# Mamba mixer with gated mixture of experts: tap order, output projection and work moved to GpSimd

## What is computed

```
def _mamba2_layer(h, Wi, cw, cb, dtb, Alog, Dh, gw, Wo):
    z, xBC, dt = split(h @ Wi)
    xBC = silu(cb + sum(xp[:, k:k + L, :] * cw[:, k] for k in range(4)))
    xs, Bm, Cm = split(xBC)
    dt = softplus(dt + dtb)
    hs = hs * exp(dt * A) + dt * xs * B     # per token, a scan
    y = (hs . C) + D * xs
    return rmsnorm(y * silu(z), gw) @ Wo

for l in range(4):
    h = h + _mamba2_layer(_rmsnorm(h, block_norm_w[l]), ...)
```

## Time and profile before

| | us |
|---|---|
| runs | 1157.63, 1160.88, 1161.12 |
| profiled execution, time | 1162.99 |
| profiled execution, span | 1161.0 |
| mean granted TensorE clock | 0.952 of full speed |
| busy PE, DVE, ACT, POOL | 993.7, 977.1, 884.2, 676.3 |

### The profile page before, as it was taken

How to read it: one execution, slowest core, us unless ns; L and a number is a source line. 1 busy time by engine, 2 the same in 40 slices (tenths; PEclk the granted TensorE clock), 3 DMA queues, 4 the chain that set the end, 5 groups by cost and what they waited for, 6 DMA issues and landing times.

```text
span 1161.0 us, 25184 instructions
## 1 busy us (share of the span) xinstructions
PE 993.7 (86%) x6136; PEld 559.7 (48%) x6136; DVE 977.1 (84%) x1801; ACT 884.2 (76%) x1724; POOL 676.3 (58%) x853
## 2 busy tenths in 40 slices
PE   5799999999899999999999999985788767999980
PEld 4244544445444444454445444542444445777760
DVE  6779999999999999999999998974778775888865
ACT  5688999999899999999999999984556534655640
POOL 0267577766776677656655765672244551666661
PEclk9789999999999999999999999998888888999995
DMA  5111242224222432210001000100000115676638
GB/s 141 34 34 33 89 156 86 88 87 153 91 86 87 142 102 86 78 32 22 22 23 31 22 22 23 27 7 1 19 28 28 37 33 180 223 232 226 223 116 217
DMA packets 85584, 97.84 MB, mean 84 GB/s; under 512 B 20698, under 2 KB 65888, under 8 KB 85536
## 3 DMA queue, kind: packets, MB, share of 16 engines
q1 hardware_dynamic: 80544, 88.83, 24.2%
q0 software_dynamic: 4992, 8.48, 2.2%
HBM read 59.67 MB, written 37.83 MB: 84 GB/s over the span
## 4 chain that ended last, share of the span: by engine, by line
PE 35%; DVE 26%; issue 18%; ACT 6%; POOL 3%; DVEq 2%; DMA 1%; ACTq 0%; SPq 0%; POOLq 0%
DVE cv L1354 9%; PE bank L494 4%; PE bank L562 4%; PE bank L681 2%; PE bank L667 2%; DVE M L1370 2%; PE bank L683 2%; PE bank L682 2%; DVE cv L1350 2%; PE bank L619 2%; PE bank L693 2%; PE bank L695 2%; PE bank L692 2%; PE bank L658 2%; PE bank L640 2%
## 5 line engine op out<-in xcount | busy, mean ns | idle before, releaser
L1354 DVE SCALAR_TENSOR_TENSOR cv<-bank,PAR,cv 128x511 f32<-128x511 f32 (+2 forms) x384 | 274.1, 742 | 15.7 <-ACT cv L963 2.8
L1370 DVE SCALAR_TENSOR_TENSOR M<-E,bank 128x512 f32<-128x512 f32 x256 | 168.3, 678 | 20.7 <-ACT E L951 11.4
L1679 POOL TENSOR_TENSOR yt<-yt,ti 128x384 f32<-128x384 f32 x64 | 64.0, 1000 | 203.6 <-DVE ti L1470 203.6
L494 PE MATMUL bank<-hn,WA 128*128 128x512 f32 x256 | 144.9, 649 | 41.0 <-DVE cv L1354 40.6
L951 ACT ACTIVATE E<-bank 128x512 f32<-128x512 f32 x256 | 149.0, 595 | 31.9 <-DVE M L1370 30.1
L1710 POOL DMA_INDIRECT RS<-y,XR x92 | 98.8, 1074 | 78.7 <-DVE y L1567 55.4
L1703 POOL DMA_INDIRECT XS<-stage,IDX x64 | 65.9, 1029 | 79.2 <-DVE run L1329 62.1
L1101 ACT ACTIVATE hr<-bank,W1B 128x512 f32<-128x512 f32 x92 | 63.4, 689 | 56.7 <-PE bank L683 49.8
L562 PE MATMUL bank<-M,dtx 128*32 128x128 f32 x2048 | 82.9, 279 | 15.6 <-DVE o_sb L1389 15.1
L494 PEld LDWEIGHTS bank<-hn,WA 128*128 128x128 f32 x256 | 40.6, 194 | 111.9 <-issue 74.0
L1497 DVE TENSOR_TENSOR hL<-hr,hH 128x512 fp32r<-128x512 f32 x124 | 87.1, 702 | 4.3
(11 more groups left out here) (245 smaller groups left out, 2633.8 us busy)
## 6 DMA issues: line engine op xcount, KB each, us to landing
XS<-PADT SPq DMA_DIRECT2D x32, 520.0 KB, 4.3
WA<-w_in SPq DMA_DIRECT2D x192, 64.0 KB, 1.8
W1B<-WD SPq DMA_DIRECT2D x23, 514.0 KB
W2B<-WD SPq DMA_DIRECT2D x23, 512.5 KB
WD<-WS SPq DMA_DIRECT2D x16, 512.0 KB, 2.7
XR<-XS SPq DMA_DIRECT2D x23, 260.0 KB
RW<-w_in SPq DMA_DIRECT2D x18, 256.0 KB, 4.4
WO_raw<-w_out SPq DMA_DIRECT2D x32, 128.0 KB, 3.6
```

The lines of the kernel that those rows point to most:

```text
L494: mm(bank[t % 2][:, :], WA[t][:, :], hn[:, :], start=True, stop=True).then_inc(pj_mm, 1)
L1354: stt(out=cv[t][:, s:L], in0=src[:, 0:L - s], scalar=PAR[:, bass.ds(cw + 3 - s, 1)], in1=cv[t][:, s:L], op0=ALU.mult, op1=ALU.add).then_in ...
L1370: stt(out=M[i % 4][:, :].rearrange("p (n t) -> p n t", n=4), in0=E[i % 2][:, :].rearrange("p (n t) -> p n t", n=4), scalar=1.0, in1=bank[5 ...
```

## The change

One: the first tap of x's first half, `tap(k + 1, .., 0, 0)`, is issued at the end of the body of step k, between yt and ti (ahead of the loop for step 0), and taps 1, 2, 3 of that half then stand in a row ahead of the causal product; tap (1, 2) goes behind it. Two: PE does `project_out` ahead of `project(3)`. Three: the copy of WDT, the square of h and the scaling of WO go from ACT to POOL, behind `own` and ahead of the wait for ti; the square is now that of step k + 2 instead of k + 1. SP waits for the scaling on POOL (`wos_p`). The two squares before the loop are ACT's for step 0 and POOL's for step 1. The semaphores `wdt_a`, `sqh_a`, `wos_a` are renamed `wdt_done`, `sqh_done`, `wos_p` throughout. The bodies of `tap` are the same, now with k and the parameter offset as arguments.

```diff
@@ PE
-                if A:
-                    project(3)
                 if C:
                     project_out()
+                if A:
+                    project(3)
@@ ACT, before the loop
-            norm_square(0)
+            f(WDT[:, :], PAR[:, C_WDT:C_WDT + 32], ACT.Copy).then_inc(wdt_done, 1)
+            act.wait_ge(hup, 1)
+            f(sqh[:, :], h[:, 0:L], ACT.Square).then_inc(sqh_done, 1)
@@ ACT, body
-                if N:
-                    norm_square(k + 1)
-                elif A:
+                if A and not N:
                     square_h(0)
...
                     row_exp(1)
-
-                    wait(act, s_wo, 16 * (j + 1))
-                    wait(act, out_mm, j)
-                    gw = act.snap(j // NB * NPAR + C_GW)
-                    for t in range(2):
-                        f(WO[:, t * DM:(t + 1) * DM], WO_raw[:, t * DM:(t + 1) * DM], ACT.Copy,
-                          scale=PAR[:, bass.ds(gw + t, 1)]).then_inc(wos_a, 1)
                     decay_exp(6)
@@ DVE, body
                 if A:
-                    tap(0, 0)
-                    tap(0, 1)
-                    tap(0, 2)
-                    tap(1, 1)
-                    tap(0, 3)
-                    tap(1, 2)
+                    tap(k, pk, 0, 1)
+                    tap(k, pk, 0, 2)
+                    tap(k, pk, 0, 3)
+                    tap(k, pk, 1, 1)
                 if B:
                     causal_products()
+                if A:
+                    tap(k, pk, 1, 2)
+                if B:
                     apply_decay(0)
...
+                if N and not B:
+                    tap(k + 1, dve.snap((k + 1) // NB * NPAR), 0, 0)
...
                         stt(out=yt[t][:, :], in0=conv_rows(t, odd + 1), scalar=PAR[:, bass.ds(pj + C_D + t, 1)],
                             in1=bank[6 + t][:, :], op0=ALU.mult, op1=ALU.add).then_inc(fin_v, 1)
+                    if N:
+                        tap(k + 1, dve.snap((k + 1) // NB * NPAR), 0, 0)
                     for t in range(2):
                         wait(dve, yi_mm, 2 * j + 1 + t)
...
+            tap(0, 0, 0, 0)
             steps(dve, body)
@@ POOL
+            def square_h(n):
+
+                hb = h[:, bass.ds(n % NB * L, L)]
+                wait(pool, hup, n + 1)
+                wait(pool, ms_mm, n)
+                tt(sqh[:, :], hb, hb, ALU.mult).then_inc(sqh_done, 1)
+
+            def step_weights(n):
+
+                wait(pool, dt_mm, n)
+                tt(WDT[:, :], PAR[:, bass.ds(pool.snap(n // NB * NPAR + C_WDT), 32)], ones_row[:, 0:32], ALU.mult).then_inc(wdt_done, 1)
+
+            def output_weights(n):
+
+                gw = pool.snap(n // NB * NPAR + C_GW)
+                wait(pool, s_wo, 16 * (n + 1))
+                wait(pool, out_mm, n)
+                for t in range(2):
+                    tt(WO[:, t * DM:(t + 1) * DM], WO_raw[:, t * DM:(t + 1) * DM], PAR[:, bass.ds(gw + t, 1)].to_broadcast([P, DM]),
+                       ALU.mult).then_inc(wos_p, 1)
...
                 if A:
                     own_rows(0)
                     own_rows(1)
+                if N:
+                    step_weights(k + 1)
+                if B:
+                    output_weights(j)
+                if N:
+                    square_h(k + 2)
                 if B:
...
+            pool.wait_ge(const_v, 3)
+            square_h(1)
             steps_with_weights(pool, body)
```

More of the change, by code:

```diff
@@ L200, in build @@
         s_wo, p4_in = sem("wo_in"), sem("p4_in")
-        wdt_a, hup, sqh_a, ms_mm, rb_a, hn_v = sem("wdt_a"), sem("hup"), sem("sqh_a"), sem("ms_mm"), sem("rb_a"), sem("hn_v")
+        wdt_done, hup, sqh_done, ms_mm, rb_a, hn_v = sem("wdt_done"), sem("hup"), sem("sqh_done"), sem("ms_mm"), sem("rb_a"), sem("hn_v")
         dt_mm, pj_mm, silu_a, dtc_v, dta_a, tr_mm = sem("dt_mm"), sem("pj_mm"), sem("silu_a"), sem("dtc_v"), sem("dta_a"), sem("tr_mm")
@@ L206, in build @@
         px_p, st_mm, s_v, e2_mm, e2_a, yi_mm = sem("px_p"), sem("st_mm"), sem("s_v"), sem("e2_mm"), sem("e2_a"), sem("yi_mm")
-        fin_v, fin_p, wos_a = sem("fin_v"), sem("fin_p"), sem("wos_a")
+        fin_v, fin_p, wos_p = sem("fin_v"), sem("fin_p"), sem("wos_p")
         sq_a, ss_mm, ry_a, out_mm, o_v = sem("sq_a"), sem("ss_mm"), sem("ry_a"), sem("out_mm"), sem("o_v")
@@ L313, in body @@
                     at_j = sp.snap(j // NB * (2 * DM * P))
-                    wait(sp, wos_a, 2 * j)
+                    wait(sp, wos_p, 2 * j)
                     sp.dma_start(WO_raw[:, :], rows(w_out, at_j, 2 * DM)).then_inc(s_wo, 16)
@@ L436, in _ @@
             pe.wait_ge(const_v, 2)
-            pe.wait_ge(sqh_a, 1)
+            pe.wait_ge(sqh_done, 1)
             mm(bank[0][:, :], mean128[:, :], sqh[:, :], start=True, stop=True).then_inc(ms_mm, 1)
@@ L483, in body @@
                     wait(pe, hn_v, k + 1)
-                    wait(pe, wdt_a, k + 1)
+                    wait(pe, wdt_done, k + 1)
                     wait(pe, s_v, 5 * j - 2)
@@ L506, in project_out @@
                 def project_out():
-                    wait(pe, wos_a, 2 * (i2 + 1))
+                    wait(pe, wos_p, 2 * (i2 + 1))
                     if B:
@@ L595, in body @@
                     square_mean_of_h(1)
+                if C:
+                    project_out()
                 if A:
                     project(3)
-                if C:
-                    project_out()
                 if C and not B:
@@ L616, in body @@
                 if N:
-                    wait(pe, sqh_a, k + 2)
+                    wait(pe, sqh_done, k + 2)
                     wait(pe, zc_a, k + 1)
@@ L846, in modulate_input @@
                   bias=MOD[:, bass.ds(b, 1)]).then_inc(hup, 1)
[L848 to L853, removed]
             def norm_log(n):
@@ L1335, in gate, with tap @@
                 dve.wait_ge(setup_v, 1)
+            def tap(k, first, t, s):
+                cw = first + C_CW + 4 * t
+                src = bank[t % 2]
+                if s == 0:
+                    wait(dve, pj_mm, 6 * k + t + 1)
+                    wait(dve, silu_a, 6 * (k - 1) + SILU_TURN[t] + 1)
+                    ts(cv[t][:, :], src[:, :], PAR[:, bass.ds(cw + 3, 1)], PAR[:, bass.ds(first + C_CB + t, 1)],
+                       ALU.mult, ALU.add).then_inc(tap_v[t], 1)
+                else:
+                    wait(dve, tap_v[t], 4 * k + s)
+                    stt(out=cv[t][:, s:L], in0=src[:, 0:L - s], scalar=PAR[:, bass.ds(cw + 3 - s, 1)],
+                        in1=cv[t][:, s:L], op0=ALU.mult, op1=ALU.add).then_inc(tap_v[t], 1)
             def body(k, odd, A, B, C, N):
@@ L1340, in body @@
                     pk = dve.snap(k // NB * NPAR)
[L1342 to L1355, removed]
                 def causal_products():
@@ L1408, in body @@
                 if A:
-                    tap(1, 3)
+                    tap(k, pk, 1, 3)
                     running_sum()
@@ L1413, in body @@
                 if A:
-                    tap(2, 1)
+                    tap(k, pk, 2, 1)
                 if B:
@@ L1417, in body @@
                 if A:
-                    tap(2, 2)
+                    tap(k, pk, 2, 2)
                 if C:
@@ L1426, in body @@
                 if A:
-                    tap(2, 3)
-                    tap(3, 1)
-                    tap(3, 2)
+                    tap(k, pk, 2, 3)
+                    tap(k, pk, 3, 1)
+                    tap(k, pk, 3, 2)
                     chunk_decay()
@@ L1433, in body @@
                 if A:
-                    tap(3, 3)
+                    tap(k, pk, 3, 3)
                 if B:
```

## The result

The changed kernel took **1177.78 us** (1177.66 to 1178.32, 4 runs) against 1161.0 before (1157.63 to 1161.73, 4 runs). The ratio is 1.0149, 95% interval 1.0131 to 1.0166: 1.5% slower. Its profiled execution took 1177.78 us at a span of 1175.6, 14.5 above the 1161.0 before. The mean granted clock of TensorE was 0.956 of full speed, against 0.952 before, so the clock is not the reason.

A forecast was written before the change was run, and what follows sets the result against it. The prediction saw VectorE, TensorE and ScalarE nearly full in the mixer's steps, with VectorE hardly resting and its neighbours waiting. It summed -8 (order), +23 and +3 (collision) to +18 on 1160.9, stated as 1178 us, range 1152 to 1192.

The forecast's parts named there:

- The exclusion of VectorE and GpSimd: Mixer steps: GpSimd's moved work, mainly the square, meets hn or stmp on VectorE and lengthens them; +23 and +3 us.
- the rows around 810 us: Earlier profile: VectorE's next operation on two SBUF tensors took 1.63 for 0.69, ending after GpSimd's instruction, itself 1.70 for 1.28.
- 26 us forecast: Collision on VectorE in the mixer: 23 us over 29 steps, and 3 us where own ends late.
- I take 0.8 in 29 steps: Mixer steps: GpSimd's square always meets hn or a stmp on VectorE, 0.8 us a step, +23 us.
- The extra 3 us for 8 late steps: 8 of 16 steps with weights: own ends late, so more work meets hn and both stmp; 0.4 each, +3 us.
- 8 us gained: VectorE's order: tap ahead of ti removes waits, 0.55 a pair of steps; taps in a row count 0.
- thin cover: ti's path over GpSimd to the square mean: ti ends a tap later, output's move gives back a projection; 3 us if lost.
- Is there slack behind it? No: VectorE from hn over S, yt and t00 to ti runs without a gap, so there is no slack behind the collision.
- equal spacing: VectorE taps: by the skill's rule dependent and independent ones are spaced alike, gain near 4 us; prediction held 0.90 against 0.66.
- A: Rival: the exclusion costs little, only the order counts, -8; 1153 us, from 1148 to 1157; chance 0.17.
- B: Rival: collision at its low bound, 7 to 11 us, cancels the order's 8; 1161 us; chance 0.10.
- C: Rival: GpSimd becomes the bound in the 16 steps with weights, 8 to 16 us more, 1186 to 1194; chance 0.11.

The follow-up runs named there:

- e3: The changed kernel plus one wait: GpSimd starts the moved work only after VectorE's last chunk state S; 1160.2 us, ratio 0.9985 to the kernel before.
- e1: The changed kernel with the moved work back on ScalarE, keeping the new order of taps and output projection; 1160.8 us, ratio 1.0005 to the kernel before.
- e5: The changed kernel with the moved work back on ScalarE and the first tap back behind ti; 1154.0 us, ratio 0.9946 to the kernel before.
- e8: The changed kernel with the output projection back behind project(3); 1180.2 us, ratio 1.0168 to the kernel before.
- e9: The changed kernel with only the square of h back on ScalarE; 1160.0 us, ratio 1.0002 to the kernel before.
- e6: The changed kernel with the moved GpSimd work waiting for the last S and the first tap back behind ti; 1150.9 us, ratio 0.9911.
- e4: The changed kernel with only the first tap put back behind ti; 1162.0 us, ratio 1.0012 to the kernel before.
- e11: The changed kernel with the tap between both ti, the square on ScalarE, dt and output weights on GpSimd behind the last S; 1141.9 us, ratio 0.9851.
- e10: The changed kernel with the first tap between the two ti and all moved work back on ScalarE; 1141.7 us, ratio 0.9844.

## Why the prediction was right, and where not

**The total and the direction** were right: 1178 forecast, 1177.8 measured, and slower. But two terms of the sum were each off by about 8 us, in opposite directions, and that the total came so close is luck. (The sum as written, 1160.9 + 18, is 1179 rather than 1178.)

**The exclusion of VectorE and GpSimd: right in kind.** The first stmp and hn were lengthened as the rows around 810 us said, ending 0.28 and 0.55 us after GpSimd's instruction. e3 shows it to be the cause. In the steps of the two views hn takes at most 1.10 us, under the forecast's 1.4 to 1.5; stmp passes 1, as forecast. The Trainium skill, "GPSIMD Engine Reference", section "Key points", names the same contention; the runs add the price.

**Its size: 26 us forecast, 17.6 measured** (change against e3). The step "I take 0.8 in 29 steps" was mis-sized. Heavy steps pay 24.28 - 23.47 = 0.81, as taken; light ones only 23.22 - 22.88 = 0.34. There hn ends at +1.09, not at 1.5: the square of one tensor takes 1.04 us on GpSimd, where I had put the 1.28 of a product of two tensors, and it started 0.50 us ahead of hn, where I had put 0.35. The extra 3 us for 8 late steps did not show: own ended 0.1 us before hn in all sixteen heavy steps, and all of them took 24.2 to 24.4 but the last (23.9).

**"8 us gained" by the order: wrong, 0 measured** (e1). The 0 is itself a sum of two: e5 gains 7 us by the row of taps and the output's move, which I had priced at 0, and the tap ahead of ti, priced at 8 gained, costs those 7 (e1 against e5). The failed step is the one on PE and its "thin cover". It named the path from ti over GpSimd to the square mean, and gave back to it a whole projection for the output's move. e8 shows that the move gives back about 2 us in all. So the second loop, lengthened by the tap's 0.7, became the bound, in both kinds of step, and I had priced the loss of the cover at 3 us and left it out. PE's first decays, which also wait for ti, were not in the prediction at all: 0.6 us of idle a step, new.

**"Is there slack behind it? No": half right.** It holds in the changed kernel. But even there some lies between hn and the S chain in the heavy steps, where hn's 0.27 costs 0.05 (e9); and with the tap behind ti hn is lengthened about as much, and stmp in as many steps, and the time is 1162.0. Against e6, its own version without the collision, the same collision costs 11 us; with the tap ahead 17.6. The price of a delay depends on which loop it finds longest.

**Dependent taps**: a tap on the result of the one before still starts some 0.15 us late and 0.88 to 0.90 apart, against 0.66 for independent ones, also where three stand in a row (four taps take 3.18 at 463.09, 2.72 in the earlier trace rows). The equal spacing that the prediction worked out from the Trainium skill, "VectorE: DVE Perf Modes", section "The DRAIN you can't avoid", is not what these traces show; the section itself has a next operation that is not held start earlier, and the independent taps do, 0.66 us after one of 0.74.

**The rivals.** A (the exclusion costs little) falls with hn at 1.02 and 1.09 and with e3. B (both cancel) falls with the time; e4 has its time, though not its small collision. C (GpSimd becomes the bound of heavy steps) fell as put, since GpSimd still waits 4.4 us for ti there. But it came close in one thing: what bounds the changed kernel does run over GpSimd, not by its load but by the length of its four operations behind ti, 4.8 us.

## What to carry to other kernels

Before work is moved to an idle GpSimd, look at what VectorE runs in that idle time: here an operation with two SBUF inputs ended only 0.3 to 0.55 us after GpSimd's instruction, so idle time beside such operations was not free, and one wait that shifts the work behind them took back all 17.6 us. Ask too whether the move earns anything: without a collision, e11 with three operations moved is as fast as e10 with none. The operation that another engine's chain starts from goes first and filler behind it: with the same tap ahead of both ti the kernel took 1160.8, behind them 1154.0, and between them 1141.7, where it does not delay the first ti. When two loops through a kernel are nearly equal, price a change in both, since a gain in one shows only as far as the other allows.

## What the runs showed of the hardware that was not expected

GpSimd squares a 128x512 f32 tensor in 1.04 us (the same tensor as both inputs), against 1.28 for a product or sum of two tensors. The exclusion works both ways within one step: with hn running, two weight scalings of 0.40 each took 1.21 together instead of 0.76, while hn, issued beside a product of 0.25, took 1.02 for 0.75.
